# Making the next batch's mask and W_hh's maxima piece by piece inside the preparation of an attention batch

## The reference

```python
# L0: 1.0 at the 5120 largest entries of a 512 x 512 matrix per batch, 0 elsewhere
adj = emb_s * emb_t * softmax(x) / sqrt(512)        # diagonal set to -inf
x = x + zeros.at[top_k(adj, 5120)].set(1.0)         # "the mask"
# L1: attention with 16 heads of 32, q and k normalised per head
xn = rms_norm(x, g_norm) * (1 + scale) + shift
q, k, v = split(xn @ W_qkv); q = rms_norm(q, g_q); k = rms_norm(k, g_k)
o = softmax(q @ k.T * 32 ** -0.5) @ v
x = x + (o + o @ W_out)
# L2: a GRU over the 512 positions, four sequences side by side
gi = x_t @ W_ih + b_ih; gh = h @ W_hh + b_hh
r, z = sigmoid(i_r + h_r), sigmoid(i_z + h_z); n = tanh(i_n + r * h_n)
h = (1 - z) * n + z * h                             # x = x + all h
# L3: linear interpolation of every row at places given by cond
```

## Time and profile before

| | us |
|---|---|
| median of three runs | 2369.89 |
| lowest and highest | 2364.55, 2374.69 |
| the profiled execution | 2376.74 |
| its span in the profile | 2375.0 |
| granted TensorE clock, share of full | 0.989 |

### The profile page before, as it was taken

The page is one execution under the profiler, slowest core; times in us unless marked ns, Lnnn a source line. Parts: engine busy times, 40 slices in busy tenths (PEclk is TensorE's granted clock), DMA queues, the critical chain, the costliest instruction groups (busy, mean ns, idle before and its releaser), DMA issues.

```text
span 2375.0 us, 133862 instructions
## 1 busy us (share of the span) xinstructions
PE 2198.2 (93%) x56981; PEld 1870.1 (79%) x56981; DVE 1634.6 (69%) x7407; ACT 1299.5 (55%) x5589; POOL 529.0 (22%) x2209
## 2 busy tenths in 40 slices
PE   3778989898987899999999999999999999999998
PEld 2664554545544499999999999999999999999886
DVE  7986968778669656666676666667666667666665
ACT  6755947748547455566544454454455455444443
POOL 2001020020113322233222222222222222222221
PEclk9998999999999999999999999999999999999999
DMA  5000000010000000000000000000000000000000
GB/s 197 3 2 1 1 1 1 1 53 1 1 36 19 19 4 5 5 5 5 5 5 5 9 9 5 9 9 5 9 5 10 9 5 9 9 5 14 10 5 21
DMA packets 8412, 31.70 MB, mean 13 GB/s; under 512 B 836, under 2 KB 904, under 8 KB 7560
## 3 DMA queue, kind: packets, MB, share of 16 engines
q1 hardware_dynamic: 7392, 23.07, 2.5%
q10 hardware_dynamic: 424, 0.07, 0.0%
HBM read 18.94 MB, written 4.19 MB: 10 GB/s over the span
## 4 chain that ended last, share of the span: by engine, by line
PE 74%; DVE 17%; ACT 4%; issue 3%; DMA 0%; POOL 0%; ACTq 0%; DVEq 0%; POOLq 0%
PE psum L1816 49%; PE psum L1750 7%; PE psum L1570 5%; DVE top L1185 4%; PE psum L1610 2%; PE psum L1646 2%; PE psum L1777 2%; PE psum L1664 2%; DVE region_cols L1036 2%; DVE region_cols L1020 2%; DVE region_work L1274 2%; PE psum L1630 1%; PE psum L1589 1%; PE psum L1548 1%; DVE neg_top L1187 1%
## 5 line engine op out<-in xcount | busy, mean ns | idle before, releaser
L1816 PE MATMUL psum<-parts0A,region_w_hh 128*128 128x40 f16 x12288 | 431.8, 181 | 10.0 <-DVE parts0A L1442 6.0
L1816 PE MATMUL psum<-parts1A,region_w_hh 128*128 128x40 f16 x12288 | 432.3, 181 | 7.7 <-DVE parts1A L1442 5.7
L1816 PE MATMUL psum<-parts0B,region_w_hh 128*128 128x40 f16 x12288 | 435.8, 182 | 1.9 <-issue 0.8
L1816 PE MATMUL psum<-parts1B,region_w_hh 128*128 128x40 f16 x12288 | 431.2, 181 | 2.3 <-issue 1.5
L1816 PEld LDWEIGHTS psum<-parts0A,region_w_hh 128*128 128x128 f16 x12288 | 379.3, 96 | 28.1 <-DVE parts0A L1442 10.7
L1816 PEld LDWEIGHTS psum<-parts1A,region_w_hh 128*128 128x128 f16 x12288 | 378.9, 96 | 26.8 <-DVE parts1A L1442 12.1
L850 ACT ACTIVATE mixA<-rzA 128x8 f32<-128x8 f32 x512 | 111.0, 217 | 524.6 <-DVE rzA L1397 524.5
L1816 PEld LDWEIGHTS psum<-parts0B,region_w_hh 128*128 128x128 f16 x12288 | 365.5, 96 | 6.9 <-issue 2.2
L1816 PEld LDWEIGHTS psum<-parts1B,region_w_hh 128*128 128x128 f16 x12288 | 362.0, 96 | 7.0 <-issue 2.2
L506 POOL TENSOR_SCALAR lineA<-lineA 128x8 f32<-128x8 f32 x512 | 122.7, 240 | 827.4 <-DVE lineA L1433 827.4
L1397 DVE TENSOR_REDUCE rzA<-psum 128x8 f32<-128x32 f32 x512 | 98.1, 192 | 219.3 <-PE psum L1816 213.4
(11 more groups left out here) (253 smaller groups left out, 3837.4 us busy)
## 6 DMA issues: line engine op xcount, KB each, us to landing
region_rows<-in_x_dram SPq DMA_DIRECT2D x4, 1024.0 KB, 13.3
out_dram<-region_w_b SPq DMA_DIRECT2D x16, 256.0 KB, 3.1
region_w_a<-in_L_cond_W_qkv_dram SPq DMA_DIRECT2D x1, 3072.0 KB, 23.4
region_w_hh<-in_L_cond_W_hh_dram SPq DMA_DIRECT2D x4, 768.0 KB, 6.4
region_rows<-in_L_cond_W_ih_dram SPq DMA_DIRECT2D x1, 3072.0 KB, 10.1
region_cond<-in_cond_dram SPq DMA_DIRECT2D x2, 1024.0 KB, 7.2
region_cols<-in_L_cond_W_emb_dram SPq DMA_DIRECT2D x1, 2048.0 KB, 19.3
region_w_out<-in_L_cond_W_out_dram SPq DMA_DIRECT2D x1, 1024.0 KB, 21.5
```

Source lines behind the costliest of these rows:

```text
L1816: made = e.matmul(k.slots(bank)[:, :, ch, :, 0:2], k.w16[:, 2 * read + c, part, NC * "rzn".index(g) + 2 * half + ch], k.parts[now][read][: ...
```

## The change

The same instructions are issued, save that four-instruction rows are cut into pieces; their places on DVE, ACT and POOL move. On PE nothing moves.

- For b < 3 DVE still flags the equal values at the head of the preparation and does prefix piece 0 (L1072 and L1073 for tile 0). Then the batch's own work starts. In turn 1 follow quota and prefix piece 1 (behind `dve_norm_heads`), piece 2 (behind the copy of turn (0, 0)) and piece 3 (behind the low parts of the keys). In turn 2 follow taken 0, taken 1, and taken 2 and 3 at the same three places.
- POOL's mask adds come behind `pool_keys` of tile 1 rather than tile 0.
- ACT's sums of squares move from the end of turn 1 to the middle of turn 3, between the high part of the queries and the copy of the turned stack; the square root to the end, and DVE's two row instructions likewise.
- For b = 3 the maxima of chunks 0 and 1 stay at the head; those of 2 and 3 come in turn 1, as does the maximum of all, and the scales in turn 2. The high parts of `W_hh` are made one turn later and ahead of the copy of the turned stack, the low parts and POOL's copies one turn later. POOL's maximum over the partitions comes behind `pool_keys` of tile 0 and ahead of `pool_out_adds`.

```diff
-    pool_mask(e, k, 0)
+    pool_mask(e, k, 0, range(NT))
     for b in range(B):
-        if b == B - 1:
-            e.wait_ge(s["hh_most"], NC + 1)
-            e.partition_all_reduce(k.hh[0][:], k.hh_chunk_most[:, NC:], P, bass.bass_isa.ReduceOp.max).then_inc(s["absmax"], 1)
         for t in range(NT):
             pool_keys(e, k, b, t)
-            if t == 0 and b + 1 < B:
-                pool_mask(e, k, b + 1)
+            if t == 0 and b == B - 1:
+                e.wait_ge(s["hh_most"], NC + 1)
+                e.partition_all_reduce(k.hh[0][:], k.hh_chunk_most[:, NC:], P, bass.bass_isa.ReduceOp.max).then_inc(s["absmax"], 1)
+            if b + 1 < B:
+                pool_mask(e, k, b + 1, MASK_TILES[t])
             if t == 0 and b:
                 pool_out_adds(e, k, b - 1)
...
-WEIGHT_CHUNKS = ((), (0, 1), (2, 3), ())
+WEIGHT_CHUNKS = ((), (), (0, 1), (2, 3))
+MASK_TILES = ((), range(NT), (), ())
...
         act_stack(e, k, b, t - 1, 0)
+        if b == B - 1:
+            for c in WEIGHT_CHUNKS[t]:
+                act_high_weights(e, k, c)
+        elif t == NT - 1:
+            act_row_powers(e, k, b + 1)
         act_turn_stack(e, k, b, t - 1, 0)
         act_stack(e, k, b, t - 1, 1)
         act_take_projected(e, k, b, t)
-        if b == B - 1:
-            for c in WEIGHT_CHUNKS[t]:
-                act_high_weights(e, k, c)
-        elif t == 1:
-            act_row_powers(e, k, b + 1)
-        elif t == 2:
-            act_row_roots(e, k, b + 1)
     act_turn_stack(e, k, b, NT - 2, 1)
     act_stack(e, k, b, NT - 1, 0)
     act_stack(e, k, b, NT - 1, 1)
+    if b + 1 < B:
+        act_row_roots(e, k, b + 1)
...
+def dve_while_act_stacks(e, k, b, t):
+    if b + 1 < B:
+        if t == 1:
+            dve_mask_quota(e, k, b + 1)
+            dve_mask_prefix(e, k, b + 1, (1,))
+        elif t == 2:
+            dve_mask_taken(e, k, b + 1, (0,))
+    elif t == 1:
+        dve_hh_most(e, k, 2)
+    elif t == 2:
+        dve_hh_scale(e, k)
+
+def dve_while_keys_stack(e, k, b, t):
+    if b + 1 < B:
+        if t == 1:
+            dve_mask_prefix(e, k, b + 1, (2,))
+        elif t == 2:
+            dve_mask_taken(e, k, b + 1, (1,))
+    elif t == 1:
+        dve_hh_most(e, k, 3)
+
+def dve_before_projected(e, k, b, t):
+    if b + 1 < B:
+        if t == 1:
+            dve_mask_prefix(e, k, b + 1, (3,))
+        elif t == 2:
+            dve_mask_taken(e, k, b + 1, (2, 3))
+    elif t == 1:
+        dve_hh_all(e, k)
...
     if b + 1 < B:
         dve_mask_equal(e, k, b + 1)
-        dve_mask_prefix(e, k, b + 1)
-        dve_mask_quota(e, k, b + 1)
-        dve_mask_taken(e, k, b + 1)
+        dve_mask_prefix(e, k, b + 1, (0,))
     else:
-        dve_hh_scale(e, k)
+        dve_hh_most(e, k, 0)
+        dve_hh_most(e, k, 1)
     dve_take_projected(e, k, b, 0)
     for t in range(1, NT):
         if t > 1:
             dve_turn_stack(e, k, b, t - 2, 1)
         dve_norm_heads(e, k, b, t - 1)
+        dve_while_act_stacks(e, k, b, t)
         dve_stack(e, k, b, t - 1, 0)
         dve_turn_stack(e, k, b, t - 1, 0)
+        dve_while_keys_stack(e, k, b, t)
         dve_stack(e, k, b, t - 1, 1)
+        dve_before_projected(e, k, b, t)
         dve_take_projected(e, k, b, t)
         if b == B - 1:
             for c in WEIGHT_CHUNKS[t]:
                 dve_low_weights(e, k, c)
-        elif t == 2:
-            dve_row_scales(e, k, b + 1)
...
+    if b + 1 < B:
+        dve_row_rms(e, k, b + 1)
     dve_stack(e, k, b, NT - 1, 0)
     dve_stack(e, k, b, NT - 1, 1)
+    if b + 1 < B:
+        dve_row_inverse(e, k, b + 1)
```

More of the change, by code:

```diff
@@ L436, in pool_split_ih, with pool_mask @@
     e.tensor_tensor(k.w_ih16[:, 1, c, cols], w, k.w_ih16[:, 0, c, cols], ALU.subtract).then_inc(s["ih_parts"], 1)
-WEIGHT_CHUNKS = ((), (0, 1), (2, 3), ())
-def pool_mask(e, k, b):
+WEIGHT_CHUNKS = ((), (), (0, 1), (2, 3))
+MASK_TILES = ((), range(NT), (), ())
+def pool_mask(e, k, b, tiles):
     s = k.sem
-    for t in range(NT):
+    for t in tiles:
         e.wait_ge(s["taken"], 4 * b + t + 1)
@@ L887, in dve_program @@
     dve_mask_equal(e, k, 0)
-    dve_mask_prefix(e, k, 0)
+    dve_mask_prefix(e, k, 0, range(NT))
     dve_mask_quota(e, k, 0)
-    dve_mask_taken(e, k, 0)
+    dve_mask_taken(e, k, 0, range(NT))
     dve_scales(e, k)
-    dve_row_scales(e, k, 0)
+    dve_row_rms(e, k, 0)
+    dve_row_inverse(e, k, 0)
     dve_columns(e, k, 0)
@@ L1066, in dve_mask_equal, with dve_mask_prefix @@
                            ALU.mult, ALU.add).then_inc(s["quota"], 1)
-def dve_mask_prefix(e, k, b):
+def dve_mask_prefix(e, k, b, tiles):
     s = k.sem
-    for t in range(NT):
+    for t in tiles:
         e.scalar_tensor_tensor(k.x[:, b, t], k.side[b][:, t], 0.0, k.x[:, b, t], ALU.is_gt, ALU.add).then_inc(s["prefix"], 1)
@@ L1079, in dve_mask_quota, with dve_mask_taken @@
     e.tensor_scalar(k.quota[:, b], k.bank(6, B, NT)[:, b], -1.0, float(TOPK), ALU.mult, ALU.add).then_inc(s["quota"], 1)
-def dve_mask_taken(e, k, b):
+def dve_mask_taken(e, k, b, tiles):
     s = k.sem
@@ L1085, in dve_mask_taken, with dve_row_rms @@
     e.wait_ge(s["prefix"], 8 * (b + 1))
-    for t in range(NT):
+    for t in tiles:
         e.scalar_tensor_tensor(k.eq[:, t], k.prefix[:, t], k.quota[:, b, t:t + 1], k.eq[:, t],
                                ALU.is_le, ALU.mult).then_inc(s["taken"], 1)
-def dve_row_scales(e, k, b):
+def dve_row_rms(e, k, b):
     s = k.sem
@@ L1094, in dve_row_scales, with dve_row_inverse @@
     e.tensor_scalar(k.row_rms[:, b], k.row_power[:, b], 1.0 / D, EPS, ALU.mult, ALU.add).then_inc(s["row_rms"], 1)
+def dve_row_inverse(e, k, b):
+    s = k.sem
     e.wait_ge(s["row_root"], b + 1)
```

14 lines of the change are left out of this document (9 added, 5 removed).

## The result

In runs taken in turn with the kernel before, the changed kernel takes 2382.14 us (median of 6 runs, 2380.21 to 2387.32) against 2367.56 us (6 runs, 2364.55 to 2374.69): a ratio of 1.0061, with a 95% interval of 1.0045 to 1.0076. It is 14.6 us slower; the interval stands for 10.7 to 18.0 us. The forecast was 2380.4 us, and the time lies in its range. Its median is just beyond the 0.5% that can be told from no change, the outcome that had a chance of 0.37, against 0.60 for a time inside that bound.

A forecast was written before the change was run, and what follows sets the result against it. PE, busy for 93% of the span, was taken as the bound, so only its idle time counted. Terms 3.9 + 1.9 + 1.9 + 2.8 = 10.5 us moved the median from 2369.89 to 2380.4 us; range 2366 to 2388 us.

The forecast's parts named there:

- The loop and its slack: Turns 1 to 3: chain of 11.4 us against PE's 12.2, 0.8 us spare per tile; removing the head block gains PE nothing.
- DVE beside POOL: Turn 1, b = 0 to 2: low parts beside a POOL add take 1.64 us, not 0.69; turn (1, 0) at z+35.7.
- the keys' pair: Turn 2's chain, b = 0 to 2: the keys' low parts beside the mask add released by taken 1, 1.25 us added.
- Rival A: The pieces fit: DVE and POOL don't meet and the code is there in time; sum -8.6, 2361.3 us; chance 0.13.
- b = 0 to 2: Turn (3, 0) of these preparations comes later: 3.9 us for b = 0, 1.9 us each for b = 1 and 2.
- terms listed for turn 2: Chain of 11.4 us, plus 1.25, 1.35 and 0.6, less 0.7 and 0.2: 13.4 to 13.9 us against PE's 12.2.
- the small operation: Turn 2: DVE's operation on `head_power` beside the next mask add, 0.6 us added to the chain.
- b = 3: Last preparation: gain of tile 1 behind POOL's code switch, W_hh split in turn 3; last W_out product starts later, 2.8 us taken.
- the switch: b = 3: POOL switches its code back after its maximum over the partitions, 7.0 to 7.89 us, ahead of its four adds.
- Rival B: Switch hidden, POOL ready at z+26; b = 3 ends 0.2 us sooner; sum +7.5, 2377.4 us; chance 0.15.
- another like: b = 3 of the kernel before: a second wait of PE, said to be like the one of 4.52 us.
- Rival C: New PE idle times in b = 0 to 2 bring the clock to 1.2 GHz: +4.2, 2384.6 us; chance 0.22.

The follow-up runs named there:

- no_mask_adds: Changed kernel with POOL's mask adds for b = 1 to 3 on 2 of 512 columns; preparations b = 0, 1, 2 take 63.32, 65.52 and 65.51 us.
- short_row_powers: Changed kernel with ACT's sums of squares for b = 1 to 3 over 2 of 512 columns; preparations b = 0, 1, 2 take 64.70, 67.28, 67.28 us.
- maxima_at_head: Changed kernel with all maxima of W_hh, POOL's over the partitions included, back at the head of b = 3, split still later; b = 3 takes 74.21 us.
- mask_only: Changed kernel with its b = 3 part put back as before, mask of b = 0 to 2 still in pieces; ratio 1.0038 to the kernel before.

## Why the prediction held, step by step

**The loop and its slack**: right. The idea that nothing was to be won at the head, since turn (0, 0) stands behind PE's own products, shows at z+21.15 in both kernels, and the 0.8 us of slack per tile is what the added work ran over. The forecast's points of b = 2 against the trace: turn (0, 1) z+25.95 and 25.91, turn (1, 0) 35.7 and 35.66, turn (2, 0) 49.1 and 48.87, turn (2, 1) 53.9 and 53.70.

**DVE beside POOL**: right in kind and size at the queries' pair of turn 1 (2.74 forecast, 2.77 measured). At the keys' pair I added 1.25 us and the row is 2.18 against 1.29, +0.89. `no_mask_adds` shows the term: without the adds b = 1 and 2 are 0.6 us shorter than before and not 1.6 longer (the kernel before has them, so this is a bound and no like comparison). Rival A, that the pieces fit, would have needed that.

**b = 0 to 2**: +3.4, +1.6 and +1.6 for 3.9, 1.9 and 1.9. All three were put a little high, by the 0.2 us of turn 2, and b = 0 by another 0.2 us at its end. The terms listed for turn 2 add up to 13.9 us, and the forecast went on with 13.4, the low end that it named; 13.2 were measured, since the keys' pair added 0.89 and not 1.25, and the small operation 0.35 and not 0.6. For ACT's sums of squares I gave 0.9 us in b = 0 and 0.5 in b = 1 and 2; `short_row_powers` shows 0.8 at the turns of b = 0, of which 0.46 is left at the end of its stretch, and 0.43 and 0.44.

**b = 3**: +3.3 for 2.8. The mechanism was right: POOL was ready at z+32.75 (forecast 33.5), since the switch took 6.81 us and not the 7.0 to 7.8 that I put on it. Turns (1, 1), (2, 0) and (3, 0) stood at 41.4, 53.0 and 68.6, each some 1 us earlier than I had them, and so did the last product, at z+73.7 for 74.6. It still came out above, because that product ran mostly at 1.2 GHz: I had priced that (4.0 in place of 1.8) and taken a value between. Rival B, a switch hidden at its new place, is out by the 6.81 us. Where the switch is hidden at its old place, `maxima_at_head` is 5.4 us faster in b = 3, far more than the 0.2 that I had computed for B: there POOL's four adds are also done before the gain of tile 1 is asked for, a case that I had not priced. A slip on which nothing hangs: the wait that the forecast calls "another like" the 4.52 us was 3.55 us.

**Rival C**, the clock falling in b = 1 and 2: out, the granted clock of both is 1.00. Idle times of 1.76 us did not bring it down there. But its premise, that so far only 2.9 us and more had done so, was a misreading: in the kernel before, the clock fell behind the 1.83 us at 624.99, and in the same place of the stretch before it did not (468.75, above). No bound on the idle time alone fits both. Its total of 2384.6 us was yet close to the measured one, by another way: the attention stretches. **That is the step that was missing**: I let everything outside the preparations stand as it was in one execution. They were 2.8 and 2.7 us longer in the two profiled executions of the changed kernel. With them the preparations' 10.0 become 12.8 us, inside both measured intervals (10.7 to 18.0, and 9.5 to 20.2), where the 10.5 that I forecast is just below the first. That they belong to the change is made likely by three executions and spoken against by `mask_only`; it isn't shown. The last 2 us up to the medians I can't place. And the last step, to set the sum on a median of 2369.89 from 3 runs, hid some of it: over 6 runs that median is 2367.56. So the forecast's nearness to the measured time is in part luck: the change was put 4.1 us too small, the kernel before 2.3 us too high, and the total came out 1.7 us off.

## What to carry to other kernels

Ask of a block that is to be cut up whether the turn behind it waits for it at all; if TensorE's own work stands ahead of that turn, the block is free where it is, and its pieces can only cost where they go. Treat VectorE's instructions with two SBUF inputs and GpSimd's that read SBUF as users of one shared resource, and hold GpSimd's, by a wait on VectorE's last such instruction, until VectorE reads from PSUM or has one input. Look for the stretch in which the producers idle behind TensorE and put whole blocks there: 7.0 us of VectorE's work and 6.0 of ScalarE's, moved into one, took, together with the held adds, 12.8 us off the window.
